# A two-layer feed-forward and recurrent-attention block on 8 cores: later projections pumped in eights, split exponent waits, four transpose semaphores

## What is computed

```python
def wkv(w, u, k, v):
    w_exp = -jnp.exp(w)
    def step(carry, kv_t):
        p, q, o = carry
        k_t, v_t = kv_t
        uk = u + k_t
        no = jnp.maximum(o, uk)
        A = jnp.exp(o - no)
        Bc = jnp.exp(uk - no)
        out = (A * p + Bc * v_t) / (A * q + Bc)
        wo = w_exp + o
        no2 = jnp.maximum(wo, k_t)
        A2 = jnp.exp(wo - no2)
        B2 = jnp.exp(k_t - no2)
        return ((A2 * p + B2 * v_t, A2 * q + B2, no2), out)
...
xk = x_prev + mix_k * (x - x_prev)
xv = x_prev + mix_v * (x - x_prev)
xr = x_prev + mix_r * (x - x_prev)
k = jnp.einsum('btc,dc->btd', xk, Wk)
v = jnp.einsum('btc,dc->btd', xv, Wv)
sr = jax.nn.sigmoid(jnp.einsum('btc,dc->btd', xr, Wr))
rwkv = sr * wkv(w, u, k, v)
return jnp.einsum('btc,dc->btd', rwkv, Wo)
```

## Time and profile before

| what | us |
|---|---|
| median of 2 runs (8669.28 to 8670.72) | 8670.0 |
| the profiled execution, slowest core | 8735.96 |
| its span, first to last instruction | 8734.3 |
| spans of the eight cores in it | 8596.2 to 8734.3 |
| one attention layer (q = 0), from its first transpose to the barrier behind it | about 436 |
| of that, the four chunks | about 320 |

### The profile page before, as it was taken

The page is one execution under the profiler, slowest core; times in us unless marked ns, Lnnn a source line. Parts: engine busy times, 40 slices in busy tenths (PEclk is TensorE's granted clock), DMA queues, the critical chain, the costliest instruction groups (busy, mean ns, idle before and its releaser), DMA issues.

```text
span 8734.3 us, 50358 instructions; the slowest of 8 cores (8596.2 to 8734.3 us)
## 1 busy us (share of the span) xinstructions
PE 3655.7 (42%) x15884; PEld 1616.9 (19%) x15884; DVE 2659.0 (30%) x2722; ACT 1378.7 (16%) x1985; POOL 680.9 (8%) x572
## 2 busy tenths in 40 slices
PE   0001464335353464344363544343473535353463
PEld 0000121222121121221121212231121212231121
DVE  1331302671321302572312112473302132274302
ACT  2321110222010110221010201131110201022110
POOL 0000110001010100001010101001010101000110
PEclk9999798668787888667797878776687878776798
DMA  9896243302324242302223242402233232501243
GB/s 232 281 246 154 79 116 87 57 0 87 106 83 120 82 120 85 70 0 85 76 90 120 89 110 92 91 1 68 75 109 112 90 106 84 109 1 48 83 114 102
DMA packets 1009168, 842.28 MB, mean 96 GB/s; under 512 B 638992, under 2 KB 901136, under 8 KB 989200
## 3 DMA queue, kind: packets, MB, share of 16 engines
q1 hardware_dynamic: 974224, 671.27, 28.9%
q10 hardware_dynamic: 25344, 117.45, 3.5%
q0 software_dynamic: 9344, 50.34, 2.1%
HBM read 536.89 MB, written 167.77 MB: 81 GB/s over the span
## 4 chain that ended last, share of the span: by engine, by line
PE 32%; DVE 23%; DMA 21%; ACT 9%; SPq 9%; issue 5%; DVEq 0%; ACTq 0%; POOL 0%; POOLq 0%
PE psA L532 12%; PE psA L539 11%; DMA dslab<-scr_dT 9%; SPq L60 8%; PE psA L634 7%; DVE s2v L573 3%; ACT gate_w L548 3%; DMA scr_hq<-hqb 3%; ACT u_w L551 3%; PE psA L798 2%; DVE hqi L601 2%; DVE hqb L604 2%; DMA uslab<-scr_uT 1%; DMA trow<-scr_d 1%; DVE xkb L771 1%
## 5 line engine op out<-in xcount | busy, mean ns | idle before, releaser
L634 PE MATMUL psA<-dslab,hqT 128*128 128x512 bf16 x4096 | 1094.5, 420 | 1944.5 <-DMA dslab<-scr_dT 1942.3
L532 PE MATMUL psA<-gslab,xqT 128*128 128x512 bf16 x4096 | 1024.8, 395 | 1503.8 <-DMA uslab<-scr_uT 861.8
L557 POOL TENSOR_TENSOR hbuf<-gate_w,u_w 128x512 f16<-128x512 f32 x512 | 648.6, 1267 | 6599.8 <-ACT u_w L551 6599.8
L539 PE MATMUL psA<-uslab,xqT 128*128 128x512 bf16 x4096 | 997.8, 388 | 0.0
L634 PEld LDWEIGHTS psA<-dslab,hqT 128*128 128x128 bf16 x4096 | 401.8, 105 | 2636.0 <-issue 2346.9
L532 PEld LDWEIGHTS psA<-gslab,xqT 128*128 128x128 bf16 x4096 | 383.4, 100 | 2118.3 <-issue 1781.5
L573 DVE TENSOR_REDUCE s2v<-hbuf 128x4 f32<-128x16384 f16 x16 | 275.5, 17217 | 1293.5 <-POOL hbuf L557 1293.5
L646 DVE SCALAR_TENSOR_TENSOR xres<-psA,dsc,xres 128x1024 f32<-128x1024 f32 x64 | 77.7, 1277 | 1918.9 <-PE psA L634 1918.9
L548 ACT ACTIVATE gate_w<-psA,gsc 128x512 f32<-128x512 f32 x512 | 351.9, 687 | 1799.5 <-PE psA L539 1799.3
L539 PEld LDWEIGHTS psA<-uslab,xqT 128*128 128x128 bf16 x4096 | 409.3, 100 | 512.5 <-issue 86.0
L798 PE MATMUL psA<-xkb,wkT 128*128 128x256 bf16 x1024 | 189.5, 369 | 632.1 <-DVE xkb L773 437.0
(11 more groups left out here) (214 smaller groups left out, 3143.4 us busy)
## 6 DMA issues: line engine op xcount, KB each, us to landing
gslab<-scr_gT SPq DMA_DIRECT2D x128, 1024.0 KB, 5.5
uslab<-scr_uT SPq DMA_DIRECT2D x128, 1024.0 KB, 8.0
dslab<-scr_dT SPq DMA_DIRECT2D x512, 256.0 KB, 3.0
scr_hq<-hqb ACTq DMA_DIRECT2D x64, 1024.0 KB, 3.9
xres<-x SPq DMA_DIRECT2D x4, 4096.0 KB, 13.5
mbat<-Wd SPq DMA_DIRECT2D x8, 2048.0 KB, 9.7
wbat<-Wd SPq DMA_DIRECT2D x8, 2048.0 KB, 31.5
mbat<-Wg SPq DMA_DIRECT2D x8, 2048.0 KB, 24.8
```

The costliest lines, as they stand in the source:

```text
L532: inst = nc.tensor.matmul(psum(bk_g, IW), ap2(xqT[alt], ct * TTILE + sub * P, P), ap2(gslab[sb_], ct * IW, IW), start=(ct == 0), stop=(ct ...
L539: inst = nc.tensor.matmul(psum(bk_u, IW), ap2(xqT[alt], ct * TTILE + sub * P, P), ap2(uslab[sb_], ct * IW, IW), start=(ct == 0), stop=(ct ...
L557: G.inc(nc.gpsimd.tensor_mul(ap2(hbuf, sub * II + iw * IW, IW), gate_w[sb_][:], u_w[sb_][:]))
L634: inst = nc.tensor.matmul(psum(sub * NCW + cw, CW), ap2(hqT[hb], sub * P, P), ap2(dslab[hb], cw * CW, CW), start=(ic == 0), stop=(ic == NI ...
```

## The change

Three edits. The transpose ring `qtr` has 4 semaphores in place of 6. `PUMP_N` is worked out by another formula: with `NCT` = 8 and `NLW` = 2 the old one gives 29 // 6 = 4, the new one 59 // 12 * 2 = 8. And at both pairs of exponents ACT waits for the first DVE instruction alone before the first exponent, and for the second one before the second.

```diff
-        qtr = DmaQ(nc, ctx, "qr", nc.sync, k=6)
+        qtr = DmaQ(nc, ctx, "qr", nc.sync, k=4)
...
-            PUMP_N = (3 * NCT + 3 * NLW - 1) // (3 * NLW)
+            PUMP_N = (2 * NCT * 3 + 6 * NLW - 1) // (6 * NLW) * 2
...
                     V.inc(nc.vector.tensor_tensor(a2w[:], oprev, ocur, ALU.subtract))
+                    va1 = V.c
                     V.inc(nc.vector.tensor_tensor(b2w[:], tmpw[:], ocur, ALU.subtract))
+                    S.wait(V, va1)
+                    S.inc(nc.scalar.activation(a2w[:], a2w[:], ACT.Exp))
                     S.wait(V)
-                    S.inc(nc.scalar.activation(a2w[:], a2w[:], ACT.Exp))
                     se1 = S.inc(nc.scalar.activation(b2w[:], b2w[:], ACT.Exp))
...
                     V.inc(nc.vector.tensor_scalar_min(aw_[:], dw_[:], 0.0))
+                    va2 = V.c
                     V.inc(nc.vector.tensor_scalar(bw_[:], dw_[:], -1.0, 0.0,
                                                   ALU.mult, ALU.min))
+                    S.wait(V, va2)
+                    S.inc(nc.scalar.activation(aw_[:], aw_[:], ACT.Exp))
                     S.wait(V)
-                    S.inc(nc.scalar.activation(aw_[:], aw_[:], ACT.Exp))
                     se2 = S.inc(nc.scalar.activation(bw_[:], bw_[:], ACT.Exp))
```

## The result

The changed kernel took 8643.87 us (median of 43 runs, 8604.3 to 8701.67) against 8691.56 us of the kernel before (42 runs, 8656.32 to 8783.59): ratio 0.994, 95% interval 0.9928 to 0.9953. Of 8692 us the ratio makes 52 us less, between 41 and 63; the medians themselves are 48 us apart. The profiled execution of the changed kernel took 8660.46 us, its slowest core (core 0 again) spans 8658.8 us.

The account below looks back on a forecast made before the run. DVE's work and waits in the attention chunks bound the kernel; waits of 50.1 us a layer become 41.4, with 5 us off L766 40 us in four layers, so 8670 - 40 = 8630 us, range 8590 to 8690.

Parts of the forecast that it names:

- DVE's waits in the chunks set the time: Attention chunks: DVE, busy 247 of 322 us, sets the time; its waits of 50.1 us a layer count.
- The split waits: Both exponent pairs: ACT starts earlier; per layer L893's waits go from 22.7 to 14.3 us, L923's from 17.6 to 12.7.
- Table loads: ACT in the chunks: four of a layer's L893 waits still carry a load, priced at 1.28 us without a drain.
- the 17 us of that estimate: Table loads on DVE's path: at the skill page's 2.66 us each, fewer loads would give another 17 us, 8613 in all.
- The longer pump: Chunks' first windows: V's evictions ahead of Ln delay the reciprocal by PE's clock; the wait in second windows goes.
- W: Reciprocal's wait (L939) in a chunk's first window: 2.1, 4.8 or 7.1 us by PE's clock, taken as 4.2, three a layer.
- The collision c: R's evictions delay ACT when DVE next asks for it: 0, 1.3 or 3.6 us, taken as 0.6, three windows a layer.
- L766: DVE's wait for the last R matmul: short waits go as R is done a window earlier, 5 us in all.
- The ring: Transpose ring at four semaphores: the wait is over before it starts; cost 0 to some 7 us, taken as 0.
- the prediction's own sign: In the profile after, SP does not wait on its own ring in front of a transpose; otherwise the prediction is wrong.
- Rival 1: PE keeps the high clock through V's and R's bursts: 72 us gained in all, 8598 us; chance 0.18.
- rival 2: V's and R's bursts run at the low clock to their end: 31 us slower, 8701 us; chance 0.13.

Follow-up runs that it names:

- e3: The kernel before with only the transpose ring cut from 6 to 4 semaphores; ratio 0.9987 (0.9966 to 1.0008).
- e4: The changed kernel with the transpose ring back at 6 semaphores; ratio to the kernel before 0.9919 (0.9888 to 0.9949).
- e5: The changed kernel with 24 unused matmuls added before the third V and third R groups of chunks 1 to 3; ratio to the kernel before 0.9919.
- e7: The changed kernel with eight fused operations and two copies moved ahead of DVE's wait for the first exponents; 8538.5 us, ratio to before 0.9865.

## Why the prediction was right

The forecast was 40 us less, 8630 us, a ratio of 0.9954; measured were 52 us less, with 0.9953 as the near end of the interval. Direction, size class and range held; the forecast was about 12 us too small. The forecast time of 8630 us was below the measured 8643.87 us although the gain was larger: it stood on 8670 us from two runs, where 42 runs gave 8691.56 us. Step by step, for the four layers:

- **DVE's waits in the chunks set the time.** Shown: DVE's busy time is the same, the waits shrank, and the stage's 57 us are the total's 52 within its interval.
- **The split waits.** L893 was to lose (22.7 - 14.3) x 4 = 33.6 us and lost 32.4; L923 was to lose 19.6 and lost 19.2. Split alone repeats both (57.5 and 51.1 us left). The two sizes of L893's wait are 2.34 us (up to 2.7 where R's evictions collide with it) and 1.25 us.
- **Table loads.** The loads changed windows, as the step said, and their price was 1.28 us: L893's waits before were 3.48 us with a load and 2.20 us without. The drain of about 1.38 us that the Trainium skill, ScalarE: Activation LUTs, What ACT_TABLE_LOAD costs, adds at every switch of set is not in these rows; the trace does not agree with it. The forecast's 40 us and the 17 us of that estimate would make the stage's 57 us, but by chance: what exceeds the forecast stands at other places, named in the next steps.
- **The longer pump.** The mechanism was right (V's evictions ahead of Ln, PE's clock deciding between a 2.0 us wait and longer ones), two of its terms were mis-sized. W was put at 4.2 us and measured 3.5 (mean of cores; 3.7 on core 0). The step knew a burst high throughout and one that starts low and takes 7.9 us for six groups. Its own row, 5.42 us for four groups, with two more at 0.87 us would have given 7.2 us. Measured were 58 windows with a wait of 3.3 to 3.7 us and bursts up to 7.07 us, 28 of which start high and fall, a case that the step did not have, and only 18 with the 4.8 us of the step. The collision c was put at 0.6 us for three windows a layer, 7 us in all; the second windows' first exponents show about 1 us of it (33.9 us for 12 x 2.34 + 4 x 1.24 = 33.0), which is inside L893's 58.4 us.
- **L766** lost 6.9 us on core 0, for 5.
- **L846** had no term. It lost 6.9 us on core 0 and 4 us in the mean of cores. The second window's output matmuls no longer stand behind R groups but start right after DVE's last operation of the window and a long idle time of PE; they take a little longer then. In pump alone the gain was not there, and why was not tried. One of them, in chunk 2 of the first layer, before and after:

```profile
1880.73 4.64 PE L831 MATMUL psA<-woT,rwk 128*128 128x512 bf16 x16
...
1873.99 5.09 PE L831 MATMUL psA<-woT,rwk 128*128 128x512 bf16 x16 [24.43 <-DVE stQ L949]
```

- **The ring.** No cost at four that e3 (0.9966 to 1.0008) and e4 can tell. The step's reason, that the wait is over before it starts, held but for late landings: by the prediction's own sign, a wait of SP on its ring, it was wrong in the small, by three waits and 2.6 us on core 0, within the 0 to 7 us that it named. At two the ring costs 1.2%, as the landing time over the issue time says.

Summed on core 0: forecast -33.6 - 19.6 + 11.2 (W) + 7.2 (c) - 5 = -40; measured -32.4 (with c in it) - 19.2 + 4.9 - 6.9 - 6.9 = -60.5, for 59.1 us by which core 0's chunks stage shrank. The four misses, at W, c, L766 and L846, all lie on one side; none made up for another. Rival 1 (high clock throughout, 72 us) is what e5 and e7 made true by other means; rival 2 (low clock throughout) was near only in single windows.

What stays open: the worth of the longer pump in total time, -6 or +4 us in the stage by what stands beside it, is below what these runs resolve. And what sets the clock of a single burst, where the length of PE's idle time just before it does not, was not tried.

## What to carry to other kernels

Where one engine's chain is the bound and another makes a pair of values for it, wait for each value alone, and look for what the chain can do without either: splitting gave 51 us of the chunks stage here, filling the wait 77 more (17.7 of them by the clock). Work that is queued in portions on a helper engine should be sized by the time to the helper's next urgent instruction at each place (8, 6 and 10 here), not evenly. And a price for matmul bursts has to name the clock at which they start, which an edit elsewhere can change by shortening or lengthening PE's idle time before them.

## What the runs showed of the hardware

- Adding 24 idle matmuls ahead of a burst shortened it from 8.11 us in the row shown to 5.40 us and the stage by 15 us. With idle times of 1.8 us in the mean the V bursts ran at the high clock throughout in 94 of 96 windows, with 3.7 us in 20, with 4.3 us in none; within one kernel the longer idle time was not the worse one (3.60 to 3.79 us for the 20, 2.83 to 3.52 us for bursts that started low).
- The ring of DMA semaphores cost time where its depth times the issue interval (1.35 us) is below the landing time (4.2 us): at depth 2 (2.7 us) 104 us of waits on the weights, at depth 4 (5.4 us) 2.6 us of waits in all and no difference in time to depth 6. Depth 3 was not run. With fewer in flight the issues themselves were shorter: 41.0 us for 32 at depth 2, 50.0 at depth 4 and 46.4 at depth 6.
- A table load cost 1.28 us and no more: the wait behind it was 3.48 us for 2.20 us without. What the removal of 24 loads is worth by itself is not shown, since in the same kernel V's evictions moved ahead of Ln.
